# Scale columns of the first modulation section made directly from narrow products in an adaLN attention and expert-FFN block

## What is computed

```python
mod = (silu(c) @ wmod).reshape(4, 6, 1, 512)
sa, ca, ga, sb, cb, gb = (mod[:, i] for i in range(6))
ga = (2 * (ga >= 0) - 1) * maximum(abs(ga), 0.25)      # gb likewise
h = layernorm(x) * (1 + ca) + sa
x = x + ga * attention(h)       # one head of 128; q, k, v from h @ Wqkv + bqkv; output @ Wo + bo
h = layernorm(x) * (1 + cb) + sb
x = x + gb * ffn(h)             # h @ W_up.T plus a rank-8 product of the expert that the gate picks
```

## Time and profile before

| | |
|---|---|
| median of 3 runs | 181.64 us (181.44 to 181.71) |
| the profiled execution | 181.46 us, of which the span of its instructions is 179.7 us |
| TensorE matmul busy | 170.8 us, 95% of the span, 918 records |
| VectorE busy | 139.4 us, 78% |
| ScalarE busy | 90.1 us, 50% |
| GpSimd (POOL) busy | 80.4 us, 45% |
| chain of work that ended last | TensorE 68%, VectorE 10%, POOL 7%, ScalarE 6%, DMA 2% |

### The profile page before, as it was taken

The page is one execution under the profiler, slowest core; times in us unless marked ns, Lnnn a source line. Parts: engine busy times, 40 slices in busy tenths (PEclk is TensorE's granted clock), DMA queues, the critical chain, the costliest instruction groups (busy, mean ns, idle before and its releaser), DMA issues.

```text
span 179.7 us, 2828 instructions
## 1 busy us (share of the span) xinstructions
PE 170.8 (95%) x918; PEld 134.0 (75%) x918; DVE 139.4 (78%) x352; ACT 90.1 (50%) x170; POOL 80.4 (45%) x109
## 2 busy tenths in 40 slices
PE   6889999989999999999999999999999999999990
PEld 5755757878678788878867787888887878768890
DVE  1957859998969997969999839699298275989964
ACT  3375045964278894339349651713477502583100
POOL 3464201279334549041979950019694000452550
PEclk9999999999999999999999999999999999999999
DMA  4999997930041002353031753001140000001414
GB/s 160 378 387 387 387 387 145 385 106 9 0 168 71 0 2 73 96 125 122 0 117 58 201 136 75 0 0 58 60 158 22 0 2 0 0 4 58 175 48 185
DMA packets 13902, 21.32 MB, mean 119 GB/s; under 512 B 3340, under 2 KB 4112, under 8 KB 13888
## 3 DMA queue, kind: packets, MB, share of 16 engines
q1 hardware_dynamic: 13888, 21.15, 35.3%
HBM read 14.83 MB, written 4.21 MB: 106 GB/s over the span
## 4 chain that ended last, share of the span: by engine, by line
PE 68%; DVE 10%; POOL 7%; ACT 6%; issue 5%; DMA 2%; SPq 0%; POOLq 0%; DVEq 0%; ACTq 0%
PE bank L398 44%; PE bank L412 3%; PE bank L521 3%; DVE stats L1020 2%; PE bank L548 2%; DMA xs<-in_L_attn_x_dram 2%; PE bank L506 2%; ACT xn_p L845 2%; PE bank L500 2%; PE bank L572 2%; PE bank L574 2%; PE bank L503 2%; POOL rstd L1493 1%; POOL xs L1508 1%; DVE xs L1232 1%
## 5 line engine op out<-in xcount | busy, mean ns | idle before, releaser
L398 PE MATMUL bank<-wup_lo,h2hi 128*128 128x512 f32 (+1 forms) x68 | 27.3, 401 | 0.4 <-ACT h2hi L903 0.4
L884 ACT ACTIVATE xn_p<-xs,shift,rstd 128x512 f32<-128x512 f32 x16 | 13.1, 816 | 26.1 <-POOL shift L1496 26.0
L398 PE MATMUL bank<-wup_hi,h2hi 128*128 128x512 f32 (+1 forms) x68 | 25.9, 381 | 0.0
L398 PE MATMUL bank<-wup_hi,h2lo 128*128 128x512 f32 (+1 forms) x68 | 25.9, 381 | 0.0
L1493 POOL TENSOR_TENSOR rstd<-var_eps,neg_half 128x1 f32<-128x1 f32 x16 | 8.8, 552 | 37.1 <-DVE var_eps L1243 37.1
L1508 POOL TENSOR_TENSOR xs<-xs,f_gb 128x512 f32<-128x512 f32 x14 | 17.9, 1292 | 7.7 <-DVE f_gb L1297 7.7
L398 PE MATMUL bank<-h1lo,wqkv_hi 128*128 128x512 f32 x48 | 19.6, 409 | 0.7 <-DVE modT_ca L1074 0.7
L1485 POOL TENSOR_TENSOR xs<-xs,gabo 128x512 f32<-128x512 f32 x16 | 20.3, 1306 | 0.1
L398 PE MATMUL bank<-h1hi,wqkv_hi 128*128 128x512 f32 x48 | 19.0, 395 | 0.0
L398 PE MATMUL bank<-h1hi,wqkv_lo 128*128 128x512 f32 x48 | 18.9, 394 | 0.0
L1215 DVE TENSOR_TENSOR plo<-bank,phi 128x512 fp32r<-128x512 f32 x16 | 10.0, 685 | 6.7 <-ACT phi L853 6.6
(11 more groups left out here) (185 smaller groups left out, 408.7 us busy)
## 6 DMA issues: line engine op xcount, KB each, us to landing
out_dram<-xs SPq DMA_DIRECT2D x15, 256.0 KB, 2.0
stage<-in_L_wmod_dram SPq DMA_DIRECT2D x3, 1024.0 KB, 7.3
xs<-in_L_wmod_dram SPq DMA_DIRECT2D x3, 1024.0 KB, 9.5
xs<-in_L_attn_x_dram SPq DMA_DIRECT2D x3, 1024.0 KB, 7.8
stage<-xn SPq DMA_DIRECT2D x32, 64.0 KB, 2.1
xs<-in_L_attn_x_dram SPq DMA_DIRECT2D x2, 512.0 KB, 3.8
f_gb<-in_L_ffn_W_up_dram SPq DMA_DIRECT2D x1, 1024.0 KB, 11.3
gb_bc<-gates_dram SPq DMA_DIRECT2D x4, 256.0 KB, 4.2
```

The costliest lines, as they stand in the source:

```text
L398: mm = nc.tensor.matmul(dst, w, m, start=first and i == 0, stop=last and i == total - 1)
L884: nc.scalar.activation(xn2_p[:, t, :], xs[:, b, t, :], ACT.Identity, bias=shift[:, 1, t:t + 1], scale=rstd[:, 1, t:t + 1]).then_inc(S["xn2 ...
```

## The change

Instead of one wide product, rows, transposes and sums, the columns of "ca" are made directly. Each block nt of 128 features is the sum over kt of products with wmod's 128x128 tile as the stationary operand and silu(c), 4 columns, as the moving one: 4 products for each of four banks, the four blocks in banks of their own. VectorE adds 1 to each 128x4 result. TensorE runs block 0 behind the transposes of token tile 1, then tiles 2 and 3, then blocks 1, 2 and 3; the keep-warm products before the first q/k/v product are gone. In VectorE's order silu goes behind the statistics of all four tiles, the columns of blocks 0, 1 and 2 stand ahead of the first low part of h1 and block 3 behind it, and the q/k/v shift row and its column sums stand among the normalisations of batch 1. Semaphore counts follow. SP's wait for `stage` is now for the fourth block.

```diff
@@ psum_plan
-        (5, "cT"), ... (3, "x1T", 0, 3), (6, "mod", 0),
-        (7, "caT", 0), (4, "caT", 1), (4, "qkv", 0, 0), (5, "qkv", 0, 1), (7, "qkv", 0, 2), (6, "mod", 1), (0, "modT", 1),
+        (5, "cT"), ... (3, "x1T", 0, 3),
+        (5, "ca", 0), (7, "ca", 1), (4, "ca", 2), (6, "ca", 3), (4, "qkv", 0, 0), (5, "qkv", 0, 1), (7, "qkv", 0, 2), (6, "mod", 1), (0, "modT", 1),
@@ SP, wait_used(g)
-                sp.wait_ge(S["mod_psum"], g + 1)
+                if g == 0:
+                    sp.wait_ge(S["ca_psum"], NK)
+                else:
+                    sp.wait_ge(S["mod_psum"], g)
@@ TensorE
-            def first_modulation_columns(half):
-                pe.wait_ge(S["mod_rows_ready"], half + 1)
-                dst = open_bank("caT", half)
-                for nt in (2 * half, 2 * half + 1):
-                    mm = nc.tensor.transpose(dst[:, nt * P:(nt + 1) * P], mod_rows[:, 0, nt * P:(nt + 1) * P], ident[:])
-                mm.then_inc(S["modT_psum"], 1)
+            def first_modulation_columns(nts):
+
+                pe.wait_ge(mod_in["ca"], 16)
+                pe.wait_ge(S["silu_step"], 4)
+                for nt in nts:
+                    dst = open_bank("ca", nt)
+                    for kt in range(NK):
+                        mm = nc.tensor.matmul(dst[:, 0:B], raw["ca"][:, kt, nt * P:(nt + 1) * P], silu_wide[:, kt, 0:B],
+                                              start=kt == 0, stop=kt == NK - 1)
+                    mm.then_inc(S["ca_psum"], 1)
...
             first_x1_transposes((1,))
-            modulation(0)
-            first_x1_transposes((2,))
-            first_modulation_columns(0)
-            first_x1_transposes((3,))
-            first_modulation_columns(1)
-            keep_warm(bank[5], 3)
+            first_modulation_columns((0,))
+            first_x1_transposes((2, 3))
+            first_modulation_columns((1, 2, 3))
             qkv(0, (0,))
@@ ScalarE, h1_high
-                    if b == 0 and kt % 2 == 0:
-                        act.wait_ge(S["modT_ready"], 1 + kt // 2)
+                    if b == 0:
+                        act.wait_ge(S["modT_ready"], kt + 1)
@@ VectorE
-            def first_modulation_rows():
...
-            def first_columns(half):
...
+            def first_columns(nts):
+
+                for nt in nts:
+                    dve.wait_ge(S["ca_psum"], nt + 1)
+                    nc.vector.tensor_scalar(modT["ca"][:, nt, :], at("ca", nt)[:, 0:B], 1.0, None,
+                                            ALU.add).then_inc(S["modT_ready"], 1)
...
-            ln1_stats(0, (0,))
-            first_ln1_aggregate(0)
-            first_ln1_variance(0)
+            for t in range(NT):
+                ln1_stats(0, (t,))
+                first_ln1_aggregate(t)
+                first_ln1_variance(t)
...
-            for t in range(1, NT):
-                ln1_stats(0, (t,))
-                first_ln1_aggregate(t)
-                first_ln1_variance(t)
             first_ln1_normalise()
-            first_modulation_rows()
-            first_columns(0)
+            first_columns((0, 1, 2))
             h1_low(0, (0,))
-            first_columns(1)
+            first_columns((3,))
             h1_low(0, (1, 2, 3))
...
-            second_ln1_normalise()
+            second_ln1_normalise((0,))
             qkv_shift_row()
+            second_ln1_normalise((1, 2))
             qkv_shift()
+            second_ln1_normalise((3,))
             qk_low(0)
```

More of the change, by code:

```diff
@@ L52, in psum_plan @@
     order = [
-        (5, "cT"), (0, "x1T", 0, 0), (1, "x1T", 0, 1), (2, "x1T", 0, 2), (3, "x1T", 0, 3), (6, "mod", 0),
-        (7, "caT", 0), (4, "caT", 1), (4, "qkv", 0, 0), (5, "qkv", 0, 1), (7, "qkv", 0, 2), (6, "mod", 1), (0, "modT", 1),
+        (5, "cT"), (0, "x1T", 0, 0), (1, "x1T", 0, 1), (2, "x1T", 0, 2), (3, "x1T", 0, 3),
+        (5, "ca", 0), (7, "ca", 1), (4, "ca", 2), (6, "ca", 3), (4, "qkv", 0, 0), (5, "qkv", 0, 1), (7, "qkv", 0, 2), (6, "mod", 1), (0, "modT", 1),
         (1, "qb_row"), (3, "qb_col"), (6, "mod", 2),
@@ L209, in adaln_block @@
             const_ready silu_zero sa_zero pool_const eb_zero dve_const silu_step cT_psum
-            mod_psum mod_rows_ready modT_psum mod_sum_ready modT_ready
+            ca_psum mod_psum mod_rows_ready modT_psum mod_sum_ready modT_ready
             sa_ready sb_split_ready ga_bc_psum ga_bc_ready gate_step gate_col_ready gate_row_psum gates_ready
@@ L229, in emptied @@
             if kind == "mod":
-                return "mod_rows_ready", of[0] + 2
-            if kind == "caT":
+                return "mod_rows_ready", of[0]
+            if kind == "ca":
                 return "modT_ready", of[0] + 1
@@ L406, in modulation @@
                     pe.wait_ge(mod_in[s], 16)
-                if g == 0:
-                    pe.wait_ge(S["silu_step"], 4)
                 quarters = [(s, kt) for s in GROUPS[g] for kt in range(0, NK, len(GROUPS[g]))]
@@ L414, in modulation @@
                 mm.then_inc(S["mod_psum"], 1)
-            def first_modulation_columns(half):
-                pe.wait_ge(S["mod_rows_ready"], half + 1)
-                dst = open_bank("caT", half)
-                for nt in (2 * half, 2 * half + 1):
-                    mm = nc.tensor.transpose(dst[:, nt * P:(nt + 1) * P], mod_rows[:, 0, nt * P:(nt + 1) * P], ident[:])
-                mm.then_inc(S["modT_psum"], 1)
+            def first_modulation_columns(nts):
[7 more added lines that the diff above has]
+                    mm.then_inc(S["ca_psum"], 1)
             def modulation_columns(g):
-                pe.wait_ge(S["mod_rows_ready"], g + 2)
+                pe.wait_ge(S["mod_rows_ready"], g)
                 dst = open_bank("modT", g)
@@ L806, in modulation_rows @@
             def modulation_rows(g):
-                act.wait_ge(S["mod_psum"], g + 1)
-                if g >= 2:
-                    act.wait_ge(S["modT_psum"], g)
+                act.wait_ge(S["mod_psum"], g)
+                if g == 3:
+                    act.wait_ge(S["modT_psum"], 1)
                 nc.scalar.activation(mod_rows[:, g % 2, :], at("mod", g)[:], ACT.Copy).then_inc(S["mod_rows_ready"], 1)
@@ L893, in h2_high @@
                         else:
-                            act.wait_ge(S["modT_ready"], 3)
+                            act.wait_ge(S["modT_ready"], NK + 1)
                     nc.scalar.activation(h2hi[:, kt, :], at("x2T", b, kt)[:], ACT.Copy,
@@ L1043, in first_ln1_normalise, with second_ln1_normalise @@
                                             ALU.subtract, ALU.mult).then_inc(S["xn1_ready"], 1)
-            def second_ln1_normalise():
+            def second_ln1_normalise(tiles):
                 dve.wait_ge(S["ln1_rstd"], NT + 1)
                 dve.wait_ge(S["x1T_psum"], NK)
-                for t in range(NT):
+                for t in tiles:
                     nc.vector.tensor_scalar(xn1[:, t, :], xs[:, 1, t, :], moments[:, 0, t, 0:1], rstd[:, 0, t:t + 1],
@@ L1055, in add_parts @@
                 n, i = len(GROUPS[g]), GROUPS[g].index(s)
-                dve.wait_ge(S["modT_psum"], g + 2)
+                dve.wait_ge(S["modT_psum"], g)
                 parts = at("modT", g)[:].rearrange("p (n s q r) -> p n s r q", n=NK, s=n, r=QUARTER)[:, :, i, 0:B, :]
@@ L1083, in scale_columns @@
                                         ALU.add).then_inc(S["modT_ready"], 1)
-                dve.wait_ge(S["modT_ready"], 3)
+                dve.wait_ge(S["modT_ready"], NK + 1)
             def widen_sa():
@@ L1150, in h1_low @@
                     dve.wait_ge(S["h1_hi"], NK * b + kt + 1)
-                    if b == 0 and kt % 2 == 0:
-                        dve.wait_ge(S["modT_ready"], 1 + kt // 2)
+                    if b == 0:
+                        dve.wait_ge(S["modT_ready"], kt + 1)
                     if b >= TURNED:
```

## The result

| | before | after |
|---|---|---|
| median | 181.68 us (6 executions) | 184.93 us (6 executions, 183.78 to 186.93) |
| profiled execution | 181.46 us, span 179.7 | 183.78 us, span 182.1 |
| mean granted clock of TensorE, profiled execution | 1.0 | 0.989 |

The ratio is 1.0156, with a 95% interval of 1.0124 to 1.0187. The sign was forecast, the size was not: 182.2 was expected in a range to 183.0.

A forecast was written before the change was run, and what follows sets the result against it. TensorE, with hardly a hole after the opening, was taken as the bound, so the first q/k/v product's start counted: 13.89 to 14.49, +0.6 us on 181.64 gives 182.2 us, range 180.9 to 183.0.

The forecast's parts named there:

- The sign: Whole kernel: slower, at a chance of 0.63, against 0.20 for faster and 0.17 for the same.
- The clock falls (slower still): Rival: TensorE's clock falls in the thinly streaming opening, 11.5 to 14.5; 184.6 us; chance 0.10 shared with loads not overlapped.
- The sum: Opening up to the first q/k/v product: its start moves from 13.89 to 14.49, +0.6 us, at full clock.
- loads that do not overlap: Rival: narrow records on TensorE cost 0.19 us each; 184.0 us; chance 0.10 shared with the clock's fall.
- always has an instruction in hand: Reason given against a clock fall in the opening: TensorE is never without an instruction; no size given.
- Its price: Cost of a clock fall behind the opening: 4.8 us of work at half rate, +2.4 us more.
- The spacing of the narrow records: 32 narrow records on TensorE in the opening, set by weight loads: 0.112 us apart, 0.90 us a block.
- The cheap-records rival: Rival: narrow records on TensorE stand 0.067 us apart or less, giving 181.2 or 180.6 us; chance 0.20.
- The start of the first q/k/v product: End of the opening on TensorE: 14.49 against 13.89, with "ca" landing at 9.49 and VectorE's low part ending at 14.23.
- silu, the shift row and keep-warm at nothing: Opening and second norm: moving silu and the shift row and dropping keep-warm cost nothing; shift row 0.1 us at most.
- The late issue of section "sb" at nothing: SP's load queue: issue moves from 10.91 to about 14.3, landing by 25.8 before its product at 26.2; no cost.
- The digits of TensorE: Busy digits of the profile before: nines from the fourth slice to the last but one, so opening costs are paid in full.

The follow-up runs named there:

- e2: The kernel before without the three keep-warm products ahead of the first q/k/v product; 181.55 us, ratio 0.9999.
- e1: The changed kernel with 128 moving columns in each narrow product instead of 4, the added ones zeros; 182.62 us, ratio 1.0068.
- e5: The changed kernel with 32 moving columns in each narrow product instead of 4; 183.16 us, ratio 1.0109.
- e8: The changed kernel with "ca" loaded as four column blocks, each block run as its quarter lands, silu early, 128 moving columns; 180.80 us, ratio 0.9975.
- e10: The changed kernel with two keep-warm products behind block 1 and two behind block 2; 183.17, 183.18, 187.57 and 188.54 us.
- e11: The changed kernel with 128 moving columns in each narrow product and silu back in its early place; 182.50 us, ratio 1.0062.
- e3: The kernel before with only silu moved behind the statistics of all four tiles; 181.65 us, ratio 1.0012.
- e4: The kernel before with only the q/k/v shift row and its column sums among the second batch's norm; 181.44 us, ratio 0.9989.

## Why the prediction was wrong

**The step that failed** is the weighing of "The clock falls (slower still)". The sum had nothing for it. The mechanism stood there with its place (little streams from 11.5 to 14.5) and was given, together with loads that do not overlap, 0.10, outside the range. The profile shows the fall right behind that stretch, from 14.1 to 17.5, and by the mean clock all ten executions of after have one. Two reasons stood against it. That TensorE "always has an instruction in hand" does not hold: after lost the clock with TensorE busy 99%, and e2 kept it with TensorE idle for 1.43 us. That no later slice of before shows a fall says nothing, for before has no such stretch. The missing keep-warm products, named beside the narrow stream, are not the cause in before (e2). Busy time is the length of the records, and one with 4 moving columns is 0.252 us long, one with 128 is 0.275, so it does not tell how much streams. The Trainium skill ("TensorE: Matmul & The Clock Gate", Part 1) says that the gate follows how busy the engine has been and advises against idle gaps. The busy share of this profile is not that measure: e1 and after have the same share and differ in the clock.

**Its price** was put at 2.4 us, from the 4.8 us that the clock took to rise at the start. A fall lasted about 3.4 us in each of the four profiles that have one. From the first q/k/v product to the scores of batch 0 these take 14.91 to 14.97 us, and the five profiles of changed kernels without a fall (e1, e5, e8, e10, e11) 13.40 to 13.43: a fall costs 1.5 us. The median is 3.25 us over before. The parts that were seen are 1.5 for one fall, some 0.5 for the narrow form at full clock (below), the long issue on SP with 0.3 to 1.1, which the forecast did not have and which both profiles of after show, and more time at half clock in some executions. How they add up in the executions without a profile is not shown.

**The spacing of the narrow records** was right: 0.112 forecast, 0.108 measured, and e1 shows that the load sets it. The cheap-records rival fell, a spacing of 0.067 or less being nowhere seen. The Trainium skill's overhead rule ("TensorEngine Tiling (Array Packing)", Instruction Overhead), 0.025 us a record as an estimate, does not agree with the 0.108 either.

**The start of the first q/k/v product** was forecast at 14.49 and came at 14.23, since "ca" landed at 9.11 in that execution rather than at 9.49 and the first block then waited for silu. I treated one landing time as fixed. In the profiles it lies between 8.8 and 10.4 us. It matters for the comparison: in before the wide product could not start before tile 1's transposes were through (9.78), but with a later landing it follows it at once. From landing to first q/k/v product before took 4.41 us in its own profile, 4.19 in e2, 4.16 in e3 and in e4; e1 took 4.99. So where the landing is late, the narrow form costs 0.8 us at the first q/k/v product, not 0.6; with the early landing of e5 (9.28) it is 4.86, 0.45 over before's own.

**silu, the shift row and keep-warm at nothing** were right within what can be measured (e3, e11; e4; e2), but for 0.18 us that TensorE waited for silu in after, where "ca" landed at 9.11. The late issue of section "sb" at nothing was right as well: it was issued at 14.00 and landed at 22.01, and the product that uses it ran at 27.29, directly behind TensorE's own work. The digits of TensorE have an 8 in the ninth slice, where the prediction reads nines; nothing hangs on it.

In sum, at full clock the forecast was near: +0.6 forecast, +0.5 in the profiled execution of e1 (182.05 against a median of 181.56), which has no long issue on SP, and +1.06 by the medians of e1, some of whose executions may have it. The largest single part of the loss is the clock, 1.5 of the 2.3 us in the profile. The parts are not added to the last tenth: e1 streams 124 columns that after does not, and after was never seen at full clock.

## What to carry to other kernels

A swap to narrow moving operands trades stream for weight loads: 32 records at 0.108 us against 8 wide ones in 1.0 us, and a profile in which TensorE looks fully busy. Read the clock of the stretch behind it, in several executions, and not the busy share. If such a form is wanted for its order (here, because a block needs only a quarter of its section), pad the moving operand to the width that the load hides anyway, and let each block start on its own part of the load.

## What was not expected of the hardware

- TensorE's clock fell to 1.2 GHz behind 2.8 us of narrow products at 99% busy, in ten executions of ten (two in profiles, the others by the mean clock); with 128 moving columns in none of ten, with 32 in two of four.
- 1.43 us of real idle time of TensorE, in the profile of e2, did not lower it.
- The same 1 MB section landed between 6.7 and 8.2 us after its issue from one execution to the next, with nothing changed ahead of it. The opening of this kernel moves with it.
- One DMA issue on SP, 0.59 us as a rule, took 1.27 to 1.70 us in five profiles of thirteen, each time 0.02 to 0.18 us behind the start of a transfer of DMA queue q8, kind "instruction". Up to the scores of batch 2 that cost 0.3 to 1.1 us.
